# Sixty-four unread products before the first scores, and the last weighting of values moved into the output product of the unit before: a three-layer cross-attention kernel

## The reference, cut to what matters

```
q, k, v = q_in @ wq + bq, k_in @ wk + bk, v_in @ wv + bv     # 128 -> 16 heads x 64
attn = softmax(mask(q k^T) / sqrt(64))
out  = (attn @ v, heads side by side) @ wo + bo              # 1024 -> 128
x    = layer_norm(out + residual)
...
# last layer: rope(q), rope(k), no biases
x = decoder_query + (attn @ v) @ Wo
y = (x - mean(x)) * rsqrt(var(x) + 0.001) * ln_gamma + ln_beta
```

## Time and profile before

| | us |
|---|---|
| median of three runs | 513.19 |
| lowest, highest | 513.02, 515.33 |
| the profiled execution: its own time | 514.0 |
| its span, first to last instruction | 512.2 |
| TensorE busy (matmul) | 497.0 |
| VectorE busy | 428.1 |
| ScalarE busy | 376.5 |
| POOL busy | 312.6 |

### The profile page before, as it was taken

One profiled execution on the slowest core, in us unless ns is written; L12 is line 12 of the kernel. 1 busy time (PEld: TensorE's weight loads), 2 busy tenths in 40 slices (PEclk: granted clock), 3 DMA queues, 4 the chain that ended last, 5 costly groups with the idle time before them and its releaser, 6 DMA issues.

```text
span 512.2 us, 23644 instructions
## 1 busy us (share of the span) xinstructions
PE 497.0 (97%) x10248; PEld 462.5 (90%) x10248; DVE 428.1 (84%) x757; ACT 376.5 (73%) x1018; POOL 312.6 (61%) x611
## 2 busy tenths in 40 slices
PE   8999999999999999999999999899999999999995
PEld 7889999999999899999999998789999999899885
DVE  4998998888899787777877888889889988788883
ACT  6867767677787687676867676777878878788761
POOL 3536566454548653455534438878678877787735
PEclk9999999999999999999999999999999999999999
DMA  8920000000011100000000000000000000000000
GB/s 242 334 92 13 3 13 13 13 3 13 25 62 44 44 4 3 3 3 3 3 2 3 4 2 3 3 4 3 9 7 10 8 10 9 13 8 10 8 9 22
DMA packets 10198, 13.78 MB, mean 27 GB/s; under 512 B 880, under 2 KB 7408, under 8 KB 10096
## 3 DMA queue, kind: packets, MB, share of 16 engines
q1 hardware_dynamic: 10096, 12.28, 7.7%
HBM read 11.23 MB, written 1.05 MB: 24 GB/s over the span
## 4 chain that ended last, share of the span: by engine, by line
PE 88%; DVE 5%; ACT 3%; issue 2%; DMA 1%; POOL 1%; SPq 0%; POOLq 0%; DVEq 0%; ACTq 0%
PE ps_p L712 16%; PE ps_p L538 9%; PE ps_p L539 9%; PE ps_p L678 8%; PE ps_p L540 8%; PE ps_a L597 6%; PE ps_a L619 5%; PE ps_p L667 5%; PE ps_a L571 4%; PE ps_p L669 4%; PE ps_p L668 4%; PE ps_p L619 3%; PE ps_p L734 2%; DVE turn L952 2%; DMA wk_raw<-in_L_xattn_sa_wk 1%
## 5 line engine op out<-in xcount | busy, mean ns | idle before, releaser
L712 PE MATMUL ps_p<-wo,headsT 128*128 128x128 f32 x768 | 93.9, 275 | 1.7 <-DVE headsT L960 0.9
L712 PEld LDWEIGHTS ps_p<-wo,headsT 128*128 128x128 f32 x768 | 90.5, 192 | 3.3 <-ACT headsT L777 1.0
L1244 POOL TENSOR_TENSOR small<-mv,epsilon 128x1 f32<-128x1 f32 x48 | 10.4, 216 | 135.3 <-DVE mv L981 135.3
L952 DVE TENSOR_TENSOR turn<-ps_p,rope 128x1024 f32<-128x1024 f32 x64 | 76.1, 1221 | 13.1 <-PE ps_p L540 11.2
L807 ACT ACTIVATE headsT<-ps_a 128x512 f32<-128x512 f32 x60 | 32.6, 596 | 64.7 <-PE ps_a L619 64.7
L538 PE MATMUL ps_p<-xT_hi,wq_hi 128*128 128x256 f32 x192 | 58.6, 305 | 1.2 <-issue 0.8
L787 ACT ACTIVATE vv<-ps_p 128x512 f32<-128x512 f32 x96 | 55.6, 620 | 5.7 <-PE ps_p L669 4.7
L823 ACT ACTIVATE probs<-ps_a,top 128x64 f32<-128x64 f32 x256 | 55.8, 353 | 5.1 <-DVE top L1025 3.2
L1055 DVE TENSOR_REDUCE total<-probs 128x16 f32<-128x1024 f32 x48 | 58.1, 1211 | 0.4 <-ACT probs L833 0.2
L539 PE MATMUL ps_p<-xT_lo,wq_hi 128*128 128x256 f32 x192 | 54.2, 282 | 0.0
L540 PE MATMUL ps_p<-xT_hi,wq_lo 128*128 128x256 f32 x192 | 54.1, 282 | 0.0
(11 more groups left out here) (149 smaller groups left out, 1391.9 us busy)
## 6 DMA issues: line engine op xcount, KB each, us to landing
out<-y_out SPq DMA_DIRECT2D x16, 64.0 KB, 2.5
raw<-in_x_turned SPq DMA_DIRECT2D x1, 768.0 KB, 9.3
across<-in_across SPq DMA_DIRECT2D x1, 704.0 KB, 8.8
raw<-in_ctx_turned SPq DMA_DIRECT2D x5, 128.0 KB, 2.3
wq_raw<-in_L_xattn_sa_wq SPq DMA_DIRECT2D x2, 256.0 KB, 3.1
wk_raw<-in_L_xattn_sa_wk SPq DMA_DIRECT2D x2, 256.0 KB, 4.6
wv_raw<-in_L_xattn_sa_wv SPq DMA_DIRECT2D x1, 512.0 KB, 5.6
wo<-in_L_xattn_sa_wo SPq DMA_DIRECT2D x1, 512.0 KB, 6.8
```

Source lines behind the costliest of these rows:

```text
L712: last = mm(bank[:, 0:E], headsT[:, p, :, :].rearrange("r b q -> r (b q)"), wo[:, layer % 2, p, :], start=(p == 0), stop=(p == PAIRS - 1))
L952: ins = V.tensor_tensor(turn[:, j % 2, :, :].rearrange("d a (h b t) -> d a h b t", h=2, t=S), bank[:, None, :].broadcast_to([128, 2, 512]) ...
```

## The change

Two edits. In step 0, `fill_wait(64)` puts 64 products of the unit matrix `eye_bf` (64 rows, 64 columns) with 8 of its columns between the mask products and the wait for the keys. They write columns 0 to 7 of bank 3 of `ps_a`, which nobody reads, and take two of the four places by turns. In the last two steps, `fills(48)` gets two more fills, `OO` 0 and 1, which are the heads of unit 47. They are made by `weight_values(49)`, which is now called after four of the eight products of `Y` of step 48, and are emptied into `hT`, viewed in the shape of `headsT`. `fills(49)` is left with `Y` alone. Step 48 also gets the normalisation on VectorE that only step 49 had.

```diff
--- before.py
+++ after.py
@@ -119,7 +119,7 @@
 
 def fills(u):
 
-    heads = [("O", b, "D" if u >= N and b else "A") for b in range(2)] if heads_in_ring(u) else []
+    heads = [("O", b, "D" if u >= N and b else "A") for b in range(2)] if heads_in_ring(u) and u < END - 1 else []
     turn_in = [("T", 0, "AD")] if u % 2 == 0 and UNITS <= 2 * (u // 2 + 1) and projected(u) is not None and not by_head(u) else []
     values = [("V", j, "A") for j in range(2)] if attends(u) else []
     probabilities = [("P", j, turned_by(u)[j]) for j in range(2)] if turns(u) and not defers(u) else []
@@ -144,6 +144,9 @@
     if u == N - 2:
 
         return deferred + values + heads + probabilities + result
+    if u == END - 2:
+
+        return heads + probabilities + [("OO", b, "AD"[b]) for b in range(2)] + result
     if u % 2:
         return heads + values + probabilities + project + result
     return deferred + heads + turn_in + values + probabilities + project[:3] + result + project[3:]
@@ -180,7 +183,7 @@
 
 def by_vector(u):
 
-    return u == END - 1
+    return u >= END - 2
 
 
 def vector_steps(u):
@@ -469,10 +472,20 @@
 
         def head_bank(u, b):
 
-            return ring(u, head_at(u) + b) if heads_in_ring(u) else ps_a[:, 2 + b, :]
+            return ring(head_step(u), head_at(u) + b) if heads_in_ring(u) else ps_a[:, 2 + b, :]
+
+        def head_step(u):
+            return END - 2 if u == END - 1 else u
+
+        def head_name(u):
+            return "OO" if u == END - 1 else "O"
 
         def head_at(u):
-            return [n for n, _, _ in fills(u)].index("O")
+            return [n for n, _, _ in fills(head_step(u))].index(head_name(u))
+
+        def heads_of(u):
+
+            return hT[:, :, :].rearrange("r c (two b q) -> r (c two) b q", two=2, b=2) if u == END - 1 else headsT
 
         @block.sync
         def _(sp):
@@ -539,6 +552,13 @@
                 mm(dst, w[0], x[1], start=False, stop=False)
                 return mm(dst, w[1], x[0], start=False, stop=True)
 
+            def fill_wait(n):
+
+
+                for k in range(n):
+                    of = slice(64 * (k % 2), 64 * (k % 2) + 64)
+                    mm(ps_a[of, 3, 0:8], eye_bf[of, of], eye_bf[of, 0:8], start=True, stop=True, skip_group_check=True)
+
             def scores(u):
                 par, v, layer = u // 2 % 2, u % 2, u // UNITS
 
@@ -585,6 +605,8 @@
                             m = mask[of, 0 if layer == 0 else 1, u % UNITS, h ^ b:(h ^ b) + 1, :]
                             mm(ps_a[64 * b:64 * b + 64, h ^ b, :], eye_bf[of, of], m.broadcast_to([64, 8, S]),
                                start=True, stop=False, skip_group_check=True)
+                if u == 0:
+                    fill_wait(64)
 
                 if v == 0:
                     out_of_bank(u - 1, "K", 2)
@@ -609,7 +631,7 @@
                         out_of_bank(u - 1, "P", j)
                 if heads_in_ring(u):
                     for b in range(2):
-                        bank_free(u, head_at(u) + b)
+                        bank_free(head_step(u), head_at(u) + b)
                 for p in range(PAIRS):
                     for g in range(2):
                         for b in range(2):
@@ -702,14 +724,16 @@
                 elif name == "Y":
                     if heads_in_ring(u):
                         for b in range(2):
-                            out_of_bank(u, "O", b)
+                            out_of_bank(head_step(u), head_name(u), b)
                     else:
                         pe.wait_ge(headed, HEADED.at(u, 1))
                     layer = (u - 2) // UNITS
                     if u - 2 in (0, 2 * UNITS):
                         pe.wait_ge(wo_loaded, 32 if layer < 2 else 48)
                     for p in range(PAIRS):
-                        last = mm(bank[:, 0:E], headsT[:, p, :, :].rearrange("r b q -> r (b q)"), wo[:, layer % 2, p, :],
+                        if (u, p) == (END - 2, HALF):
+                            weight_values(END - 1)
+                        last = mm(bank[:, 0:E], heads_of(u)[:, p, :, :].rearrange("r b q -> r (b q)"), wo[:, layer % 2, p, :],
                                   start=(p == 0), stop=(p == PAIRS - 1))
                 elif name == "FT":
                     pe.wait_ge(pool_step, PSTEP.at(u - 2, "out", 0))
@@ -762,7 +786,7 @@
                         scores(N - 1)
                     if (name, j) == ("O", 0):
                         weight_values(u)
-                    elif name != "O":
+                    elif name not in ("O", "OO"):
                         fill(u, at, name, j)
                 if u in BIAS_STEPS:
 
@@ -773,8 +797,9 @@
             def empty(u, at, name, j):
                 bank = ring(u, at)
                 act.wait_ge(filled, FILL.before(u) + at + 1)
-                if name == "O":
-                    ins = nc.scalar.activation(headsT[:, :, j, :], bank[:, :].rearrange("r (p q) -> r p q", q=S), ACT.Copy)
+                if name in ("O", "OO"):
+                    ins = nc.scalar.activation(heads_of(u + len(name) - 1)[:, :, j, :],
+                                               bank[:, :].rearrange("r (p q) -> r p q", q=S), ACT.Copy)
                 elif name == "T":
                     g = turned_in(u)
                     ins = nc.scalar.activation(inputs_of(g)[0][0][:, :, 0:2 * S], by_unit(bank[:, 0:CT]), ACT.Copy)
@@ -956,8 +981,8 @@
                                           .rearrange("d (a h) b t -> d a h b t", a=2), ALU.mult)
                 elif name == "P":
                     ins = V.tensor_copy(probsT[:, j, :], bank[:, :])
-                elif name == "O":
-                    ins = V.tensor_copy(headsT[:, :, j, :], bank[:, :].rearrange("r (p q) -> r p q", q=S))
+                elif name in ("O", "OO"):
+                    ins = V.tensor_copy(heads_of(u + len(name) - 1)[:, :, j, :], bank[:, :].rearrange("r (p q) -> r p q", q=S))
                 elif name == "F2":
                     if ffn_chunk(u - 2) is not None:
                         dve.wait_ge(dve_step, VSTEP.at(u, "fout", 1))
```

## The result

| | before | with the change |
|---|---|---|
| median, us | 513.92 (19 runs) | 511.56 (19 runs) |
| lowest to highest | 512.44 to 517.04 | 510.55 to 512.59 |
| profiled execution, its span | 514.0, 512.2 | 512.3, 510.4 |

The ratio is 0.9947, with a 95% interval of 0.9933 to 0.9961: 2.4 us, or 0.46% by the medians and 0.53% by the ratio, faster. I had forecast 0.36. The runs also lie closer together: 2.0 us from lowest to highest, against 4.6.

What follows compares the result with a forecast made beforehand. TensorE, busy 497.0 of 512.2 us at full clock, was taken to bound the kernel, so only the two ends could matter. Filling 0 and tail 0.36 us off 513.19 gave 512.8 us, range 511.5 to 514.7.

Steps and rivals of the forecast that it cites:

- The filling: Step 0, the 64 products between mask products and scores: hidden behind the wait for keys, cost 0.
- F: Length of the 64 products in step 0, taken as 0.92 us; it delays the value product by F - 1.24.
- Rivals 1 and 2: Step 0: each place needs 57.5 ns, F 1.84, 513.4 us, chance 0.17; or serial loads, F 3.30, 514.9 us, chance 0.08.
- The tail: Last two steps: the last weighting inside the output product of step 48 brings the last z 0.36 us earlier.
- the rest of the kernel is as before: End of the tail's working: the last z comes 0.36 us earlier and nothing else in the kernel changes.
- rival 4: The filling holds the clock in runs where it was lost: say 1.5 us more, 511.3 us, chance 0.07.

Runs made afterwards that it cites:

- the tail alone: The change without its 64 products in step 0, against the kernel before: 514.87 us against 515.64, ratio 0.9994.
- the run with 32 and 64: The change with 32 products in step 0 in place of 64, and 64 more in step 31: 512.66 us, ratio 0.9975 to the kernel before.

## Why the prediction was wrong

At the two places that the prediction spoke of, TensorE and VectorE went as it said, up to the start of the last y_out:

- **The filling.** F was 0.96 (forecast 0.92), the value product 0.01 later against the mask products (forecast 0). 15.0 ns for a product that takes turns with one other place is under the 25 ns that the Trainium skill states in "TensorE: Matmul & The Clock Gate" (section "Wait — 56ns, not 53.3ns?") for any width, so here the measurement speaks against the page. Rivals 1 and 2 fell with it.
- **The tail.** All counted from the weighting of unit 46: Y of step 48 at 2.44 (forecast 2.54), the last weighting at 3.52 (3.51), the other half of Y at 4.61 (4.61), the last Y at 5.62 (5.60), the last z at 7.91 (7.84), behind VectorE's own y_out as said. The last y_out came 0.30 earlier, forecast 0.36. My own figures gave 0.32: with VectorE free at 507.64 the last z could not start at 507.60. The end of the kernel came 0.00 earlier, since 0.29 are lost behind the last store.

**The step that failed** is the one at the end of the tail's working, "the rest of the kernel is as before", together with the price of the 64 products as no more than their time on TensorE. Neither what lies behind the last y_out nor the middle was as before. I counted what an added instruction takes and not that it moves all that follows it in TensorE's instruction stream. The kernel before held pauses for it, and they were there to be read: the page gives q8 81 packets and the waits of TensorE list "issue" where no engine was late. I took the middle as one block, at 97% busy with "almost nothing to win". All of the 1.85 us in the span came from there: 0.99 lost up to z of step 36, 2.33 won to z of step 46 and 0.50 more to the weighting of unit 46. The ratio of the tail alone is 0.9994.

The measured 511.56 lies just inside my range of 511.5 to 514.7. That is luck: only rival 4 reached so low, and the median of the kernel before came out at 513.92, not 513.19.

**Rival 4** had the size, 1.5 us more, and the wrong cause. The clock was at the top in both traces, and with the wait of step 0 empty and the products at the start the gain was the same. The spread that I took as a sign of it (515.33 against 513.19) does shrink with the change, from 4.6 to 2.0 us. Pauses that differ from run to run would explain this, and that they differ is seen in two traces: the kernel before and the one with the tail alone have the same instructions on TensorE up to step 48, but only the second pauses for 1.41 us at 335.0. Over many runs it was not traced.

What stays open is the length of a pause: it hangs on when the packet starts, and for that no rule was found. So the ends can be counted out beforehand, and the pieces that run through in under about 3 us, but not what each will cost (the run with 32 and 64 had 1.88 us at one that nobody expected, and the changed kernel 0.37 at 381.6 behind a piece of 4.4 us). What the views draw as idle is also less than the loss: idle of TensorE in z 36 to z 46 is 2.19 us before and 0.80 after, by the busy times of the two stretches (stage, length, TensorE busy first):

```profile
390.33:494.64 104.31, 102.12 (x2643) 93.77 (x2630) 88.59 (x120) 82.00 (x286) 76.35 (x111) 1.00 0.04 10
```

```profile
391.32:493.29 101.97, 101.17 (x2674) 93.95 (x2664) 88.60 (x119) 81.67 (x286) 76.37 (x111) 1.00 0.04 10
```

The other 0.95 is drawn as busy time; by the comparison product by product it stands at the ends of the pieces too.

## What to carry to other kernels

In a long unrolled program, adding or taking away instructions on the busiest engine moves everything behind them against the ends of the fetched pieces, and that alone was worth up to 0.5% here, more than both edits were by their own working. So when an edit gains or loses where it changed nothing, compare distances between like events along the whole trace, look for "issue" waits, and set them beside the starts of the instruction queue's packets. Count the engine's records modulo 256: if the pauses share one remainder, they are ends of pieces; most of those here stood behind 256 instructions that took 3.1 us or less. Then shift the stream by half a piece elsewhere before you credit the edit. Where small instructions are put into a wait, count them as well as time them: 128 products with their 128 loads in 2 us can run ahead of the fetching, and then the filling makes the pause. And follow a gain at the end of a kernel to the last instruction of the span: here 0.30 us at the last y_out were nothing at the end.

## What the runs showed of the hardware that was not expected

- TensorE's instruction pauses stand at one remainder of its record count modulo 256 (193, 46 pauses in 13 traces), 39 of them behind 256 records run through in 1.4 to 3.1 us: 0.2 to 1.1 us in the last layer, 1.24 and 3.54 us in the first 23 us, where the input loads run beside the fetching (DMA busy share 1.02 to 1.06), 1.41 us at 335.0 us in the kernel with the tail only, and 1.88 us at 334.9 us in that with 32 and 64, both where 128 score records with their 128 loads take 1.5 us.
- Such a pause can cost the clock too: behind the 3.54 us the granted clock was 0.53 over 7 us, behind the 1.88 us it was 0.65 over 4 us. Behind those of 1.24 and 1.41 us it stayed at 1.00.
- Products of 8 columns on two places by turns start every 15.0 ns while the clock is full (12.63 to 13.59). At the start of the kernel, ahead of the warming products, the same 64 took 1.80 us to the next product (1.91 to 3.71), 28 ns each. The ten warming records behind them take 216 ns each (3.71 to 5.87), and records of that form in Y 122 ns, so the array was slower there, though the view gives a granted clock of 1.00 for that stretch too.
